# Three bf16 parts of queries and keys split in the accumulator by a negative identity, biases folded, values copied by ScalarE

## What is computed

```python
qkv = x @ qkv_w + qkv_b
local = softmax(mask(q @ k.T * scale)) @ v          # window of 128, the token itself left out
pooled = x.reshape(B, 64, 8, D).mean(axis=2)
rq = x @ rq_w + rq_b ; rk, rv = split(pooled @ rkv_w + rkv_b)
remote = softmax(mask(rq @ rk.T * lscale)) @ rv @ rout_w + rout_b
gate = sigmoid(local @ gl_w + remote_h @ gr_w)
mixed = gate * local + (1 - gate) * remote_h
x = layernorm(x + mixed @ out_w + out_b)
h = gelu(rmsnorm(x) @ ternary(w_up).T)
x = layernorm(x + rmsnorm(h) @ ternary(w_down).T)
```

## Time and profile before

| | |
|---|---|
| three runs, us | 1172.92, 1170.47, 1173.93; median 1172.92 |
| the profiled execution, us | 1173.3 |
| its span, from the first to the last instruction, us | 1171.6 |
| mean granted clock of TensorE | 0.926 of full speed |

### The profile page before, as it was taken

How to read it: one execution, slowest core, us unless ns; L and a number is a source line. 1 busy time by engine, 2 the same in 40 slices (tenths; PEclk the granted TensorE clock), 3 DMA queues, 4 the chain that set the end, 5 groups by cost and what they waited for, 6 DMA issues and landing times. The chain is left out here.

```text
span 1171.6 us, 36746 instructions
## 1 busy us (share of the span) xinstructions
PE 982.2 (84%) x15202; PEld 634.5 (54%) x15202; DVE 933.7 (80%) x1928; ACT 686.3 (59%) x1093; POOL 703.8 (60%) x881
## 2 busy tenths in 40 slices
PE   5768898989988898998889898888988888884855
PEld 3445564656556565555646555565656555562523
DVE  6479879797988978798897979889897978875554
ACT  3424665657576565757656575756656576662544
POOL 7205765565667566566756656675665667673664
PEclk8879999999999999999999999999999999996787
DMA  7730604325070522507043340705234150601000
GB/s 220 204 103 27 172 30 120 100 66 154 5 215 4 153 67 75 144 4 216 3 136 83 86 134 4 216 4 163 57 101 119 48 153 4 187 16 37 1 20 18
DMA packets 58179, 107.50 MB, mean 92 GB/s; under 512 B 19718, under 2 KB 38038, under 8 KB 54934
## 3 DMA queue, kind: packets, MB, share of 16 engines
q1 hardware_dynamic: 57868, 105.15, 32.1%
q10 hardware_dynamic: 144, 0.00, 0.0%
HBM read 70.93 MB, written 33.55 MB: 89 GB/s over the span
## 5 line engine op out<-in xcount | busy, mean ns | idle before, releaser
L824 ACT ACTIVATE Pt<-scores 128x1024 f32<-128x1024 f32 (+1 forms) x256 | 230.0, 917 | 147.7 <-PE oacc L1508 83.7
L1091 DVE TENSOR_REDUCE nmax<-work 128x3 f32<-128x480 f32 x352 | 215.6, 634 | 37.0 <-PE work L1462 33.7
L677 POOL TENSOR_TENSOR h_lo<-hbuf,h_hi 128x512 f16<-128x512 f32 x128 | 148.0, 1156 | 157.4 <-DVE h_hi L1222 157.4
L649 POOL TENSOR_SCALAR_AFFINE_SELECT Pt<-Pt 128x512 f32<-128x512 f32 x256 | 164.1, 641 | 99.8 <-ACT Pt L824 99.2
L1508 PE MATMUL oacc<-Pt,Vp 128*32 128x256 f32 (+1 forms) x2048 | 155.7, 362 | 15.2 <-POOL Pt L653 8.5
L1457 PE MATMUL work<-Ks,Qs 98*32 98x160 bf16 x4096 | 150.4, 240 | 16.1 <-DVE nmax L1091 11.7
L636 POOL TENSOR_TENSOR parts<-Pt,parts 128x512 bf16<-128x512 f32 x64 | 72.9, 1158 | 136.0 <-ACT parts L749 136.0
L1488 PE MATMUL scores<-Qs,Ks 100*32 100x160 bf16 (+4 forms) x4096 | 126.9, 239 | 29.7 <-ACT Pt L824 14.1
L1521 PE MATMUL oacc<-wdn_t,h_hi 128*128 128x256 f16 x512 | 125.5, 283 | 18.0 <-POOL h_lo L677 18.0
L1488 PEld LDWEIGHTS scores<-Qs,Ks 100*32 100x32 bf16 x4096 | 87.8, 102 | 77.8 <-ACT Pt L824 47.6
L1521 PE MATMUL oacc<-wdn_t,h_lo 128*128 128x256 f16 x512 | 125.4, 283 | 0.0
(11 more groups left out here) (159 smaller groups left out, 1910.2 us busy)
## 6 DMA issues: line engine op xcount, KB each, us to landing
parts_scratch<-parts SPq DMA_DIRECT2D x96, 256.0 KB, 5.3
Qs<-parts_scratch SPq DMA_DIRECT2D x96, 256.0 KB, 5.1
Ks<-parts_scratch SPq DMA_DIRECT2D x96, 256.0 KB, 4.8
xT<-x_t SPq DMA_DIRECT2D x16, 512.0 KB, 6.7
xres<-x SPq DMA_DIRECT2D x16, 512.0 KB, 7.7
y<-nat SPq DMA_DIRECT2D x16, 512.0 KB, 3.1
Qs<-nmax_pair SPq DMA_DIRECT2D x256, 2.0 KB, 1.7
nat<-up_t SPq DMA_DIRECT2D x1, 1024.0 KB, 7.7
```

What stands on the lines that cost most here:

```text
L649: ins = pool.affine_select(out=pt[:, :, 0:P], in_=pt[:, :, 0:P], compare_op=ALU.is_gt, fill=0.0, base=0, pattern=[[0, 4], [1, P]], channel ...
L677: pool.tensor_tensor(h_lo[:, t % NR, :], hbuf[:, t % 2, :], h_hi[:, t % NR, :], ALU.subtract).then_inc(h_lo_ready, 1)
L824: nc.scalar.activation(Pt[:, u % NPT, :, 0:w], scores[:, slot, :, :].rearrange("p k (h q) -> p (k h) q", h=2)[:, :, 0:w], ACT.Exp, scale=S ...
L1091: nc.vector.tensor_reduce(nmax[:, first:first + n], work[:, slot, 0:n * BAND].rearrange("p (h c) -> p h c", h=n), X, ALU.max, negate=True) ...
```

## The change

- The quarter's product stays in its bank. ACT rounds it to part 0, PE adds minus the identity times part 0 into the same bank (`minusb`, bf16), ACT rounds what is left to part 1, PE subtracts again, ACT rounds to part 2. Eight new steps per sequence, SPLIT to SPLIT + 7 (two per quarter), stand in the table. Lines 1018, 749 and 636 are gone, and a bank is held until its part 2 is out.
- ACT copies the values out of the accumulator (in all four VALUES steps); DVE's add is gone.
- The value bias is folded: into the output bias, the remote bias, the gate's bias and the first token's row (`dead`). DVE transposes the remote part straight from the accumulator, ACT's copy is gone, and POOL adds the remote bias minus the value bias in place, two instructions of 128x512 (`bias_remote`), behind its four for the residual. DVE's gate waits for that (`rem_biased`).
- The low half of the normalised activations is made the same way as the parts: PE adds minus the high half (`minus`, fp16), ACT rounds.
- `split_maxima` moves from the end of the first half to behind step UP + 1, and `move_max` behind `restack` on SP, except before the last sequence.
- The prologue issues nine more loads, and makes the folded biases.

```diff
 SECOND_HALF = (
-    ("F", GATE), ("P", QK), ("P", QK + 1), ("P", QK + 2), ("F", OUT), ("P", QK + 3),
-    ("F", OUT + 1), ("P", LAT_RQ), ("P", LAT_RKV), ("P", VALUES), ("P", LAT_SCORES), ("F", NORM),
+    ("F", GATE), ("P", QK), ("P", QK + 1), ("P", SPLIT), ("P", QK + 2), ("P", SPLIT + 1), ("P", SPLIT + 2),
+    ("F", OUT), ("P", QK + 3), ("P", SPLIT + 3), ("P", SPLIT + 4), ("F", OUT + 1), ("P", SPLIT + 5), ("P", SPLIT + 6),
+    ("P", LAT_RQ), ("P", SPLIT + 7), ("P", LAT_RKV), ("P", VALUES), ("P", LAT_SCORES), ("F", NORM),
...
 def body(s):   # SyncE
-                if not s.last:
+                if s.i == B - 2:
                     move_max(s.next())
...
                 if later.exists:
                     restack(later)
+                    move_max(s.next())
...
 GpSimd
-                    pool.tensor_tensor(parts[:, 2, t, :], qk_rest[:, t, :], parts[:, 1, t, :],
-                                       ALU.subtract).then_inc(part2, 1)
...
+            def bias_remote(s):
...
+                for t in range(KT):
+                    ins = pool.tensor_tensor(rem[:, s.par, t, :, :], rem[:, s.par, t, :, :],
+                                             rem_b[:, t, :].unsqueeze(1).to_broadcast([P, G32, 2 * HD]), ALU.add)
+                ins.then_inc(rem_biased, 1)
...
                 for b in range(NB):
                     add_bias(s, b)
-                later = s.second_next()
+                if s.next().exists and not s.first:
+                    bias_remote(s.next())
...
 ScalarE
-                if k == LAT_RQ and s.i >= 2 or QK <= k < QK + 4 and s.i < 2:
...
-                        nc.scalar.activation(parts[:, 1, t, :], qk_rest[:, t, :], ACT.Copy).then_inc(part1, 1)
+                if SPLIT <= k < SPLIT + 8:
+
+                    t, j = (k - SPLIT) // 2, (k - SPLIT) % 2 + 1
+                    bank, n = p_use(s, 2 + t)
+                    act.wait_ge((rest1, rest2)[j - 1], count(s, 4, t))
+                    nc.scalar.activation(parts[:, j, t, :], p_bank(bank), ACT.Identity, bias=bqk[:, t:t + 1]
+                                         ).then_inc((part1, part2)[j - 1], 1)
+                    if j == 2:
+                        act.wait_ge(part2, count(s, 4, t))
+                        act.sem_inc(p_taken[bank], 1)
...
+                if VALUES <= k < VALUES + NB:
...
+                if k == XN_LO:
+                    for t in range(KT):
+                        act.wait_ge(xn_rest, count(s, KT, t))
+                        nc.scalar.activation(xnT[:, 1, t, :], oacc[:, t, :], ACT.Copy).then_inc(xn_lo, 1)
...
 VectorE
+                    dve.wait_ge(rem_biased, count(s, 1, 0))
                     for i in range(2):
                         mark(nc.vector.tensor_tensor(
                             mixed[:, i, :, :].rearrange("p t (k d) -> p t k d", d=HD),
...
 TensorE
+                if SPLIT <= k < SPLIT + 8:
+
+                    t, j = (k - SPLIT) // 2, (k - SPLIT) % 2
...
+                    pe.wait_ge((part0, part1)[j], count(s, 4, t))
+                    nc.tensor.matmul(p_bank(bank), minusb[:, :], parts[:, j, t, :], start=False, stop=(j == 1),
+                                     skip_group_check=True).then_inc((rest1, rest2)[j], 1)
```

215 lines of the change are left out of this document (114 added, 101 removed).

## The result

The changed kernel takes 1198.28 us (median of four runs, 1196.89 to 1200.37); the kernel before, run beside it, 1171.7. The ratio is 1.0232, with a 95% interval of 1.0199 to 1.0266: slower by 2.3%. The forecast was 1192.0, the range 1168 to 1211. The profiled execution took 1197.75 us, its span is 1196.0 against 1171.6 before.

The account below looks back on a forecast made before the run. Bound: no single engine, but a chain changing between PE, DVE and ACT. 1.3 us per period over 13 sequences (16.9), less 0.3 for sequence 0, plus 2 of prologue, gave 18.6 on 1173.3: 1192 us; range 1168 to 1211.

Parts of the forecast that it names:

- The gate: Last PV product to `mixT`: POOL's additions hold DVE's two-input operations, `mixT` 1.5 us late, bounds 0.9 and 1.8.
- the second hold: In the gate: POOL holds DVE's small operations behind the tanh to 792.1, so line 1161 starts at 792.8.
- waits for them by the new semaphore: 0.9 us late at least: In the gate: DVE's mixing (line 1161) waits until POOL's two remote additions end at 792.2, at least 0.9 us late.
- only the semaphore: Rival, chance 0.15: only the semaphore delays the gate, `mixT` 0.9 us late, 0.7 per period, 1184 us.
- `mixT` to the latent scores: PE and ACT behind the gate: 10.3 us against 10.4 before, the saved detour eaten by the splits' round trips.
- Up to the third quarter the ladder costs nothing more: PE/ACT split round trips (the ladder): PE's third quarter waits for tanh and part 0, but still ends ahead of `mixT`.
- my own test: Wrong if the normalisation starts more than 0.5 us from 0.25 late; then the split round trips were mis-walked.
- To the first gelu: Normalisation 1.0 us behind the latent scores, not 2.2; four more ACT instructions cost 1.4; gelu 1.7 late.
- Behind the gelu: First gelu onward: moved `split_maxima` loses 0.5 us, dropped remote copies gain 0.9; together -0.4, bounds -0.9 and +0.5.
- The prologue: Before the first scores: nine more loads cost 4 us, about 2 given back; +2, bounds -3 and +6.
- PE's lower clock: Rival, chance 0.12: PE falls to its lower clock in the split steps, 1.3 us more per period, 1209 us.
- The "faster" rival: Rival, chance 0.15: POOL's additions finish before DVE needs them or ACT's steps fit better; -0.5 us per period, 1167 us.

Follow-up runs that it names:

- e1: The changed kernel with POOL's two remote-bias additions issued behind the normalised blocks instead of ahead of the gate: 1170.22 us, ratio 1.0004 to the kernel before.
- e2: The changed kernel with the low halves of the normalised activations again subtracted on DVE, without the identity product and ACT's copies: 1186.55 us.
- e3: The changed kernel with the copies of the value banks moved from ACT to DVE, the bias still folded: 1206.13 us.
- e10: The changed kernel with the split of the maxima and its transfer back at their old place, ahead of the gate: 1194.92 us in one run.
- e4: The changed kernel with the old chain of query and key parts (DVE remainder, ACT copy, POOL subtraction) instead of the SPLIT steps: 1230.28 us.
- e8: The changed kernel with nine of twelve steps of sequence 1's parts moved between sequence 0's maximum products in the prologue: 1200.49 us, one run.
- e5: The changed kernel with the edits of e1 and e2 together: 1152.91 us, ratio 0.9850 to the kernel before.
- e7: The changed kernel with POOL's two remote operations reading one source (adding constant 0), remote bias left out, for timing only: 1179.95 us, one run.
- e11: e5 with POOL's four output-bias additions moved out of the gate: two behind later low halves, two behind the sequence's last power: 1150.38 us.
- e9: e5 with the residual loaded one sequence sooner and POOL's output-bias additions moved, two behind the remote ones, two behind the last power: 1341.92 us.
- e6: e5 with the output bias put into the output banks by PE products instead of POOL's four additions: 1175.81 us.

## Why the prediction was right, and where its parts were not

The sign, the place of the main loss and the mechanism of the gate and of ACT's queue held. The sum came near partly by luck. By the first gelu the period was 2.97 us late (1.97 + 0.84 - 1.16 + 1.32) where I had 1.7, and behind it 1.49 us came back where I had 0.4: two errors of more than 1 us each that cancelled.

- **The gate: right in mechanism, one mechanism too many.** DVE's operations with two SBUF inputs stood still beside POOL's additions, and e1 shows that this is the whole loss. `mixT` came 1.97 us late, not 1.5, above my upper bound of 1.8. That each POOL instruction holds DVE's chain once was right. What I misplaced is the second hold: I walked it to the small operations behind the tanh, with the tanh 0.8 late. Both fell ahead of it, the tanh was 1.97 late, and nothing more was lost behind it (3.54 us to `mixT`, as before). The additions of POOL also took 1.26 us each where I had 1.158. The step "waits for them by the new semaphore: 0.9 us late at least" was wrong: that count is reached a sequence earlier. So the first rival, "only the semaphore", had nothing under it.
- **`mixT` to the latent scores: 11.19, I said 10.3.** "Up to the third quarter the ladder costs nothing more" held in ten sequences of thirteen and failed in three, where the clock fell: 0.34 us in the mean. From the first output product to the end of the second it was 5.87, where my terms make 5.91. The rest was 4.98 against 4.39: two splits 0.54 (said 0.45), latent queries 1.08 (0.9), the last split 0.75 (0.75), part 2 0.72 (0.65), queries and `lat_bd` 1.88 (1.64). Most of them were taken a little short. By my own test, the normalisation within 0.5 us of 0.25 late, I was wrong: behind the last PV product it came 1.65 late. Of the 1.4 between them 0.5 is the gate, 0.8 to 0.9 the ladder, the rest the next stage.
- **To the first gelu: right.** 1.10 to the normalisation (said 1.0), 6.96 from there (said 7.2). The mechanism, ACT's queue without a gap, is shown by e2 and by e3's 0.58.
- **Behind the gelu: -1.13, I said -0.4.** The split of the maxima cost 0.37 (said 0.5), so -1.5 is left. Of that, 0.33 is the value additions that left DVE, by e3, which puts them back as copies. Some 0.6 is PE's clock, below. The remaining 0.6, by elimination the remote copies that left ACT, was not tested by itself.
- **Left out: the attention stage, -0.36.** 0.20 of it is again the clock, below. The rest can't be told from the scatter, and e10 shows no share of the split's move.
- **The prologue: +5.6, I said +2, bounds -3 and +6.** The cause was not the one I priced. The loads do make the value products later (29.76 in e4, 26.16 before), but by the first scores that is gone. e4 shows that the new chain of parts costs it all. In the change's trace PE waits four times there for ACT's parts, 5.82 us together, which fits; but e8 moved most of sequence 1's turns and won nothing, so which of them sets the time stays open.
- **PE's lower clock: nothing in my sum, a rival of 0.12, and it worked both ways.** In sequences 1, 5 and 10 the rival came true: behind PE's wait of 2.33 us (2.51 in one) the clock falls at the third quarter, which cost 0.29 us per period in the mean, not the rival's 1.3. OUT is late in this way in two to four sequences of e2, e3, e8 and e10 too, and in none of e1, e5, e7 and e11, so it goes with the ladder behind a late tanh. First two stretches of the change in sequence 10, the third quarter and the one ahead of the gelu (PE, PEld, DVE, ACT and POOL busy, then the granted clock, DMA share and GB/s), which was at 0.76 before:

```profile
809.60:812.70 3.10, 3.06 (x5) 1.05 (x6) 3.03 (x6) 1.91 (x4) 0.00 (x0) 0.60 0.05 16
826.00:832.20 6.20, 5.26 (x27) 3.24 (x26) 2.44 (x4) 6.18 (x12) 1.61 (x2) 1.00 0.75 213
```

Then from the last gelu to the next S product: the kernel before behind sequences 7 and 10, the change behind sequence 10:

```profile
624.76:630.96 6.20, 4.88 (x44) 3.17 (x41) 3.83 (x9) 2.48 (x3) 3.10 (x3) 0.80 0.01 3
827.94:833.02 5.08, 3.76 (x45) 2.69 (x42) 3.48 (x7) 2.48 (x3) 3.05 (x3) 1.00 0.00 0
847.64:852.29 4.65, 4.07 (x48) 3.20 (x46) 3.05 (x6) 2.48 (x3) 2.25 (x3) 1.00 0.65 213
```

Before, the clock fell there in eight of thirteen sequences, and they took 5.79 to 6.21 us; the others took 5.09 or less. In the change it stayed at 1.00 in all. So of the 1.00 us that this stage won, 0.6 is the clock and 0.4 is shorter work. Where the clock was still low at the start of the next attention, the first exponential came at up to 0.78 us instead of 0.51: 0.20 in the mean. Over the span the clock rose from 0.926 to 0.96, where the rival wanted it lower. Which edit ended these falls was not tested.

Term by term, behind the attention stage: +1.97 + 0.84 - 1.16 + 1.32 - 1.13 = 1.84, less 0.36 of attention: 1.48. I had 1.3. The "faster" rival was the right picture of everything but the gate: without POOL's additions in it (e1) the period is 66.84, under the 67.50 of before, and with the low halves back on DVE (e5) it is 65.63.

## What to carry to other kernels

Work that nobody waits for can still cost: two additions on an idle engine, beside another engine's chain of small operations with two SBUF inputs, cost 28 us here, and a later place in the same queue gave it all back. A place further off is not free by itself: in e11 the moved additions met another small operation of DVE. So when work goes to POOL, look at what DVE does at that moment, not only at who needs the result. And before moving an operation forward, look at what it waits for and who stands behind it in its queue (e9); a gain in one stretch counts only after the next one has been read too (e3, e6, e11). Read more than one sequence: sequence 10, shown here, is one of three with the clock low at the third quarter, and one of five with its pattern in the gate.

## What the runs showed of the hardware that I had not expected

- POOL's two-source additions hold even the smallest DVE operation with two SBUF inputs up to the end of the POOL instruction: 1.15 to 1.30 us for an addition of 128x32 that takes 0.19 in e1, 1.27 for one of 128x64 that takes 0.26 in e11. Each of the two remote additions held one operation of the chain. The reciprocal in the same chain, with one input, took 0.55 us beside POOL's additions of the output bias and 0.55 in e11, where no POOL addition runs there: not held. But one input is no safety by itself: e11's addition of a constant to 128x4 is held, 0.70 us against 0.17.
- With one source on POOL (e7) the hold is partial: 609 ns in the mean for the addition of 128x64, which takes 379 in e1 and 262 in e11, and 227 for those of 128x32, against 188. The Trainium skill, "SBUF — State Buffer", section "SBUF: two separate sides", says that VectorE and GpSimd share a port pair as an exclusive lock, which whichever starts first has for the whole instruction, and that a VectorE operation with two SBUF inputs meets it beside any GpSimd operation that reads SBUF. For two sources the trace agrees (DVE freed at 808.50, POOL's end at 808.45). For one source the records show two-input operations that end within POOL's instruction, so there the measurement speaks against the whole instruction.
- A product of one row by 512 columns in fp32 costs PE 0.99 us, as one of 128 rows does.
